# Maxima laid into the query strips by DMA, and transposed scores in one pass, in the second attention of a two-layer kernel

## The reference

```python
nx = _layernorm(x, ln1_w, ln1_b)
qkv = nx @ Wqkv + bqkv                       # 16 heads of 16
scores = jnp.einsum('bqhd,bkhd->bhqk', q, k) / jnp.sqrt(jnp.float32(HEAD_DIM))
scores = jnp.where(causal, scores, jnp.finfo(scores.dtype).min)
attn = jax.nn.softmax(scores, axis=-1)
out = jnp.einsum('bhqk,bkhd->bqhd', attn, v).reshape(B, S, D)
x = x + out @ Wo + bo
```

## Time and profile before

| | us |
|---|---|
| median of 3 runs | 1744.22 |
| lowest, highest | 1743.34, 1748.14 |
| profiled execution | 1746.09 |
| its span | 1744.2 |
| PE busy in the span | 1620.8 (93%) |
| DVE busy | 1146.9 (66%) |
| ACT busy | 899.1 (52%) |
| POOL busy | 378.7 (22%) |

### The profile page before, as it was taken

How to read it: one execution, slowest core, us unless ns; L and a number is a source line. 1 busy time by engine, 2 the same in 40 slices (tenths; PEclk the granted TensorE clock), 3 DMA queues, 4 the chain that set the end, 5 groups by cost and what they waited for, 6 DMA issues and landing times.

```text
span 1744.2 us, 32605 instructions
## 1 busy us (share of the span) xinstructions
PE 1620.8 (93%) x11293; PEld 1109.7 (64%) x11294; DVE 1146.9 (66%) x2716; ACT 899.1 (52%) x1970; POOL 378.7 (22%) x447
## 2 busy tenths in 40 slices
PE   8998989889999877999998889999999999989998
PEld 6555545445555565999995444665666666567887
DVE  4776767656555377444445778877766776867776
ACT  2887878635555543444443557756665665720000
POOL 1111111322453221111111321432323231210000
PEclk9999999989999978999998999999999999999999
DMA  8787778543233164556563311100100010020001
GB/s 299 262 289 258 253 260 289 185 66 60 46 58 64 54 217 146 201 192 205 199 211 102 91 41 34 55 13 25 36 24 27 13 31 25 2 85 1 1 0 48
DMA packets 89023, 194.72 MB, mean 112 GB/s; under 512 B 10592, under 2 KB 53216, under 8 KB 84416
## 3 DMA queue, kind: packets, MB, share of 16 engines
q1 hardware_dynamic: 85488, 183.75, 33.6%
q0 software_dynamic: 3408, 9.31, 1.7%
HBM read 129.19 MB, written 51.25 MB: 103 GB/s over the span
## 4 chain that ended last, share of the span: by engine, by line
PE 79%; DVE 10%; ACT 6%; issue 3%; DMA 1%; DVEq 0%; SPq 0%; POOL 0%; ACTq 0%; POOLq 0%
PE PS L1555 10%; PE PS L1391 8%; PE PS L1510 6%; PE PS L973 5%; PE PS L1426 5%; PE PS L1525 5%; PE PS L1500 5%; PE PS L1374 4%; PE PS L1040 4%; PE PS L1062 3%; PE PS L1481 3%; PE PS L1151 2%; PE PS L1073 2%; PE PS L1376 2%; PE PS L1123 2%
## 5 line engine op out<-in xcount | busy, mean ns | idle before, releaser
L1984 ACT ACTIVATE P<-PS,nm 128x512 f32<-128x512 f32 x256 | 174.6, 695 | 108.5 <-DVE nm L2592 87.3
L1510 PEld LDWEIGHTS PS<-idf,P 128*128 128x128 f32 x1024 | 118.0, 143 | 101.9 <-issue 69.9
L2185 DVE CUSTOM_DVE_ANT_0 SN<-PS,SR 128x128 f32<-128x128 f32 (+3 forms) x256 | 115.4, 488 | 92.8 <-PE PS L1044 92.7
L1510 PE MATMUL PS<-idf,P 128*128 128x128 f32 x1024 | 155.9, 282 | 15.5 <-ACT PTb L1994 13.9
L2247 DVE TENSOR_REDUCE mxs<-PS 128x2 f32<-128x512 f32 (+3 forms) x128 | 105.5, 824 | 96.7 <-PE PS L1137 96.4
L2592 DVE TENSOR_REDUCE nm<-PS 128x2 f32<-128x1024 f32 x128 | 150.4, 1215 | 24.7 <-PE PS L1500 23.9
L1391 PE MATMUL PS<-xT,W1c 128*128 128x128 f32 x1248 | 145.9, 275 | 2.8 <-ACT xT L1909 1.8
L1391 PEld LDWEIGHTS PS<-xT,W1c 128*128 128x128 f32 x1248 | 142.6, 192 | 5.0 <-ACT xT L1909 2.3
L1843 ACT ACTIVATE PTf<-PS 128x1024 f32<-128x1024 f32 (+3 forms) x128 | 89.3, 704 | 87.0 <-PE PS L1125 86.8
L1726 ACT ACTIVATE SN<-SN,nm 128x128 f32<-128x128 f32 (+3 forms) x256 | 128.8, 555 | 7.0 <-DVE nm L2185 6.9
L2812 DVE SCALAR_TENSOR_TENSOR X<-PS,gat,X 128x256 f32<-128x256 f32 x224 | 97.0, 479 | 46.2 <-PE PS L1555 45.3
(11 more groups left out here) (364 smaller groups left out, 3577.7 us busy)
## 6 DMA issues: line engine op xcount, KB each, us to landing
W1c<-in_fc1T SPq DMA_DIRECT2D x39, 1024.0 KB, 5.3
SR<-rel SPq DMA_DIRECT2D x16, 1024.0 KB, 7.7
rel<-EN SPq DMA_DIRECT2D x15, 1024.0 KB, 4.8
SR<-rel SPq DMA_DIRECT2D x16, 768.0 KB, 6.8
rel<-EN SPq DMA_DIRECT2D x15, 768.0 KB, 4.3
SR<-rel SPq DMA_DIRECT2D x16, 512.0 KB, 4.2
W2f<-in_fc2T SPq DMA_DIRECT2D x8, 1024.0 KB, 8.1
rel<-EN SPq DMA_DIRECT2D x15, 512.0 KB, 3.3
```

Source lines behind the costliest of these rows:

```text
L1510: last = nc.tensor.transpose(TR1[j][:, c * P:c * P + P], P1[s % 4][:, j, c * P:c * P + P], idf[:])
L1984: last = af(P1[s % 4][:, j, :], PD[s % 2][:, j, :], ACT.Exp, bias=nm1[:, s % 4, j:j + 1], accum_out=sm1[:, s % 4, j:j + 1])
L2185: v.tensor_tensor_reduce(SN[k % 6][:, 0:w], SB[k % 3][:, 0:w], SR[r][:, 2 * pr + i, :], -1.0, -LOW, ALU.add, ALU.min, nm[:, k % 16:k % 16 ...
```

## The change

The maxima are now laid into rows of the query strip itself (`max_strip_rows`): two transfers on SyncE's queue take four rows of `MS` each, twice side by side, to `QD`. So the one matmul with `KD` takes the maxima off as well, and the second pass over `MS` is gone. The natural scores use only the 48 rows in front of them. The transposed scores of a job wait for these transfers (semaphore `f_ml`) and not for ScalarE's copy. `AHEAD` becomes 14, `FIRST_G` 0; values, maxima, projections and outputs stand in other steps; the strips are issued in another order, the maxima of the next job behind the strips of this one.

```diff
-AHEAD = NUF + 4
+AHEAD = NUF + 6
 F_ROWS = (1, 1, 0, 0, 3, 3, 2, 2)
-V_STEPS = {2: (0,), 3: (1, 2), 4: (3,)}
-MX_STEP, OT_STEP = 6, 7
+V_STEPS = {2: (0,), 3: (1, 2, 3)}
+MX_STEP, OT_STEP = 4, 7
...
-           (2, 4): [(("h", 6), 1)], (3, 4): [(("h", 7), 1)]}
+           (2, 5): [(("h", 6), 1)], (3, 5): [(("h", 7), 1)]}
 for _b in range(1, B):
-    for _i, _u, _use in ((4, 0, ("hk", _b, 0)), (4, 4, ("hk", _b, 1)), (3, 0, ("hq", _b, 0)), (3, 4, ("hq", _b, 1)),
-                         (2, 0, ("hv", _b, 0)), (1, 0, ("hv", _b, 1))):
+    for _i, _u, _use in ((4, 0, ("hk", _b, 0)), (4, 5, ("hk", _b, 1)), (2, 0, ("hv", _b, 0)), (1, 0, ("hv", _b, 1))):
         for _p in range(2):
             H_PARTS[4 * _b - _i, _u + _p] = [(_use, _p)]
+    for _x in range(2):
+        H_PARTS[4 * _b - 3, _x] = [(("hq", _b, _x), _p) for _p in range(2)]
...
-FIRST_G = 5
+FIRST_G = 0
...
+            def max_strip_rows(n):
+                m_done(sp, ("mx", n))
+                for x in range(2):
+                    rows = slice(HS * x + DQ, HS * x + DQ + DM)
+                    sp.dma_start(QD[n % NQD][rows].bitcast(F32),
+                                 MS[n % 2][rows].bitcast(F32).unsqueeze(1).to_broadcast([DM, 2, S])).then_inc(f_ml, 16)
...
-            for m in range(2, NJ):
+            for m in (2, 3):
                 key_strips(m)
-                query_strips(m)
-                if m == HGS:
+                if m < NQD - 1:
+                    query_strips(m)
+                else:
+                    max_strip_rows(0)
+            for n in range(NJ):
+                k, q = n + NKD - 1, n + NQD - 1
+                if k < NJ and k % HGS:
+                    key_strips(k)
+                if q < NJ:
+                    query_strips(q)
+                if n + 1 < NJ:
+                    max_strip_rows(n + 1)
+                if k < NJ and k % HGS == 0:
+                    key_strips(k)
+                if n == 0:
...
-                    if c == 2 and n + 1 < NJ:
+                    if c == 1 and n + 1 < NJ:
                         place_max(n + 1)
...
                     if u == 0:
-                        m_done(pe, ("mx", n))
+                        pe.wait_ge(f_ml, 32 * n + 32)
...
-                        mm(bank(x), keys(x), QD[n % NQD][HS * x:HS * x + HS, t, c * P:S], start=True, stop=False)
-                    for x in range(2):
-                        last = mm(bank(x), keys(x), MS[n % 2][HS * x:HS * x + HS, c * P:S], start=False, stop=True)
+                        last = mm(bank(x), keys(x), QD[n % NQD][HS * x:HS * x + HS, t, c * P:S], start=True, stop=True)
                     last.then_inc(f_st, 1)
...
-                        mm(NB[:, x, 0:w], QD[m % NQD][HS * x:HS * x + HS, y, r * P:r * P + P],
-                           KD[m % NKD][HS * x:HS * x + HS, y, 0:w], start=True, stop=False, skip_group_check=True)
+                        mm(NB[:, x, 0:w], QD[m % NQD][HS * x:HS * x + DQ, y, r * P:r * P + P],
+                           KD[m % NKD][HS * x:HS * x + DQ, y, 0:w], start=True, stop=False, skip_group_check=True)
...
                 if n >= 2:
-                    act.wait_ge(f_st, (n - 1) * NUF)
+                    act.wait_ge(f_ml, 32 * n - 32)
...
-                    if u == 4 and n:
+                    if u == 3 and n:
                         copy_out(n - 1)
```

More of the change, by code:

```diff
@@ L529, in build @@
         f_mx = sem("f_max_placed")
+        f_ml = sem("f_max_rows_loaded")
         strip_sem = {"k": a_w[0] + [sem("f_keys_loaded4")], "q": a_w[1]}
```

## The result

| | median us (lowest to highest, runs) | ratio to before [95%] |
|---|---|---|
| before | 1746.18 (1743.34 to 1751.88, 4) | |
| after | 1786.72 (1784.52 to 1788.21, 4) | 1.0227 [1.0197, 1.0257] |

The change makes the kernel 2.3% slower, 40.5 us. The prediction had the sign right and the size wrong: 1759, with 1770 as the upper end.

What follows compares the result with a forecast made beforehand. It took a TensorE-VectorE loop of naturals and maxima through one bank pair as the bound. Hand-over +13.3, steady jobs +3, job 0 -0.9, tail 0 gave +15.4 us: 1759 on the median, range 1753 to 1766, 1748 to 1770 with nearer rivals.

Steps and rivals of the forecast that it cites:

- The loop of naturals and maxima: Second attention: TensorE and VectorE alternate through one bank pair, 2.03 us per 512-wide natural, at least 12.3 us a job.
- Hand-over, +13.3: First to second attention: late last output delays constants, strips and first maxima; transposed scores start at 397.1 instead of 383.83.
- the five links: Hand-over signs: last tmpA 378.7, GpSimd constants to 382.7, KD strips from there, first maxima transfer 394, transposed scores from 397.
- the constants don't hold SyncE: Hand-over rival, 10%: SyncE's queue is ready in time, the stage starts only 4.2 us later, total 1750.
- The two more naturals: Hand-over: two more 512-wide naturals are done before the first transposed scores, claimed hidden in the wait there.
- The landing, 2.3 us from issue: Maxima transfers: land 2.3 us after issue (bounds 2.2 to 3.6), hidden in plain jobs, some 0.7 late in query-projection jobs.
- The steady jobs, +3: Jobs 1 to 13: query jobs 1.3 us longer three times, key jobs 0.4 shorter twice, the rest about 0.
- the naturals' wait for maxima: Sign in the second attention's trace: TensorE's wait for VectorE's maxima grows from 16 to well over 30 us.
- Job 0, -0.9: First job of the second attention: narrower naturals in steps 0 and 1 and no second pass, estimated -0.9 us.
- The tail, 0: Jobs 14 and 15: about -2 for the lost pass and naturals, +2 for job 15's wait for maxima, sum 0.
- TensorE's queue is the limit: Rival on the second attention's jobs, 10%: all 20.8 us of the pass come back, net -7.5, total 1737.
- The maxima land late in every job: Rival, 8%: transfers take 3.6 instead of 2.3 us, adding 0.3 to 1 in each of 14 jobs; about 1770.

Runs made afterwards that it cites:

- e2: The changed kernel with FIRST_G back at 5, so fewer naturals run inside the first attention: 1775.30 us, ratio 1.0170.
- e10: The kernel before with one line changed, naturals running 14 steps ahead instead of 12, both passes kept: 1757.61 us, ratio 1.0068.
- e12: e4 plus 13 filler matmuls a job (128x128, output never read): 1748.95 us, ratio 1.0025.
- e13: e12, but job 0 takes its maxima off with the old pass over MS and transfers begin with job 1: 1750.58 us, ratio 1.0018.
- e14: e2, with the change's own natural rows, plus 13 filler matmuls a job: 1758.15 us, ratio 1.0062.
- e7: The kernel before without its pass over MS and nothing in its place, so maxima are not taken off: 1741.58 us, ratio 0.9990.
- e9: The kernel before with one line changed, the values lumped in steps 2 and 3 instead of 2 to 4: 1749.87 us, ratio 1.0033.
- e4: e2 with the widths of the naturals in each step put back as before: 1768.40 us, ratio 1.0120.
- e11: e4 with the values spread over steps 2, 3 and 4 as before: 1776.20 us, ratio 1.0160.
- e8: e2 with before's steps (AHEAD 12, values, outputs, projections), maxima still over DMA, their transposes in step 4: 1802.74 us, ratio 1.0348.

## Why the prediction was right and wrong

- **The loop of naturals and maxima: right.** 2.03 us between 512-wide naturals (584.21 to 586.24), 48 rows no faster than 64 where the loop decides.
- **Hand-over, +13.3: right.** The scores start 12.4 us later (396.19 against 383.83), the first exp 11.9; as the first attention was 1.5 faster in this execution, the hand-over itself takes 13.5 to 13.9. Each of the five links that were to be looked for is there; the rival in which the constants don't hold SyncE is refuted by the KD strips at 381.67. e2 gives 9 to 11 us for the naturals' place. The two more naturals, which I had hidden in the wait, cost some 4 once that place is undone (e10, e12 and e13: the first exp 3.9 to 4.1 later against the issue of the query strips).
- **The landing, 2.3 us from issue: right.** The second issue is half of 1.50 behind 392.99, so at about 393.7, and the scores start at 396.19, 2.45 later; the trace has no landing of these transfers itself. That they would be in time in plain jobs and late behind query projections: right. From 400 to 590 the scores wait twice, 1.70 and 0.53 us, behind the query projections of jobs 1 and 9.
- **The steady jobs, +3: the step that failed.** Measured +25.6 for jobs 1 to 13, of +29.4 for the stage. The sum itself holds: at clock 1.00 (e14) a plain job takes 13.50, a query job 15.75, and jobs 1 to 13 are 3.4 over before's. What failed is that every piece was priced at the clock of the rows it was read from. I compared steps by which of loop and TensorE ends them, and wrote "loop, 2.03 each" for steps 6 and 7 without asking what TensorE does in those 2.03 us, and whether it keeps its clock then. The clock was 0.84 where it had been 1.00, and with the rows as the change has them that costs 17 us in the median (e2 against e14), 22 in the stage.
- **A sign that failed:** the naturals' wait for maxima was to grow from 16 to well over 30 us. It is 20.3 in after, and 19.0 in e10, which has the longer lead at clock 1.00; why it grew so little was not looked into.
- **Job 0, -0.9:** -0.3 in after, +1.2 in e14, whose fillers may have a share in it.
- **The tail, 0: too little.** +1.8 at clock 1.00, +4.1 in after. The scores of job 15 wait 1.60 us for their maxima in after (634.02) and 1.59 in e14, about the +2 of the prediction; the -2 set against it did not come.
- **The rivals.** "TensorE's queue is the limit" would give 1.3 us a job; e7, without the pass, has 0.7 less in a job at clock 1.00 and as good as nothing in the whole. "The maxima land late in every job" came nearest with 1770, but by another cause. The rival that was missing is the clock.
- **Still open:** what in the order brings the clock down. The values alone do it in part (e9), the lead alone does not (e10), the pass has a share (e7), and giving the rows their old places takes off 7 us (e4). e11 went against what I expected, and its trace doesn't say why.

## What to carry to other kernels

When work is taken from an engine whose clock follows its activity, or its order is changed, look in the new order for the stretch of some microseconds in which TensorE has the least to do, and price the dense part behind it at the low clock as well. Filler matmuls are a cheap test of a suspected clock, but they must be few: 13 a job brought back 17 to 20 us here, 24 to 29 only 3 to 12. A longer lead is paid at the start of the stage, in instructions that must run ahead of the first use (here 4 us for two more naturals). And before a transfer is put behind others on a queue, ask what those wait for: in e8 the strips ahead of the maxima held them for 6 us, three times.

## What the runs showed of the hardware that was not expected

- Thirteen added matmuls a job take 17 to 20 us off the kernel (e12, e14); in the job shown of after, the clock falls although no idle time in it is longer than 1.06 us.
- The clock can fall with no thinner 2 us than a kernel has that keeps it (e9: 1.23 us of matmuls in the least busy one, as before), and stay with a thinner one (e10: 1.03).
- Jobs with the same work can differ by 2 us in one execution: 14.43 and 16.43 with a key projection, 17.40 and 15.75 with a query projection in after, where before has 14.39 and 14.40, 14.69 and 14.68. The plain ones take 15.3 to 16.8 and before 13.39 each.
- A transfer of 16 KB over four rows costs SyncE more to issue than a strip of 64 KB over 16 (two take 1.44 to 1.50 us, six strips 3.7 to 3.8: 0.72 to 0.75 against 0.61 to 0.63 each).
